# Expert tiles of 384 slots instead of 512, fifty of them instead of thirty-nine

## What is computed

```python
xn = layernorm(x)
# mixer: in-projection, causal convolution of 4 taps, silu, a linear recurrence along the sequence, out-projection
mixed = mixer(xn)
# experts: 8 of them, the best two for each token
logits = xt @ w_gate
top_logits, sel = top_k(logits, 2)
probs = softmax(top_logits)
h = silu(einsum('td,edh->eth', xt, w1)) * einsum('td,edh->eth', xt, w3)   # 128 -> 256
y = einsum('eth,ehd->etd', h, w2)                                         # 256 -> 128
out = einsum('ktd,tk->td', y[sel.T, t_idx], probs)
return x + mixed + out
```

## Time and profile before

| what | us |
|---|---|
| median of 3 runs | 543.55 (541.63 to 545.46) |
| the profiled execution, its own time | 539.55 |
| its span, first to last instruction | 537.7 |
| what lies around the span | 1.85 |

### The profile page before, as it was taken

How to read it: one execution, slowest core, us unless ns; L and a number is a source line. 1 busy time by engine, 2 the same in 40 slices (tenths; PEclk the granted TensorE clock), 3 DMA queues, 4 the chain that set the end, 5 groups by cost and what they waited for, 6 DMA issues and landing times.

```text
span 537.7 us, 8279 instructions
## 1 busy us (share of the span) xinstructions
PE 455.9 (85%) x2118; PEld 322.9 (60%) x2118; DVE 446.7 (83%) x947; ACT 313.6 (58%) x380; POOL 326.8 (61%) x317
## 2 busy tenths in 40 slices
PE   0668797778888889887999999999999998888863
PEld 0666663344434444444888888888888885444343
DVE  5898859899999999995977667667777765999996
ACT  1224236788888988886444444444444435888970
POOL 1047777788887868400477777777777777842210
PEclk9996668989999999998999999999999999899986
DMA  9501111951111111122466656666566640079995
GB/s 249 136 27 51 56 51 54 162 95 47 41 41 41 42 39 41 55 75 59 122 177 174 181 164 190 167 175 189 168 186 187 185 126 17 0 129 174 235 236 165
DMA packets 72599, 63.26 MB, mean 118 GB/s; under 512 B 9418, under 2 KB 64878, under 8 KB 72576
## 3 DMA queue, kind: packets, MB, share of 16 engines
q1 hardware_dynamic: 61184, 37.50, 27.1%
q0 software_dynamic: 11392, 25.53, 18.0%
HBM read 39.50 MB, written 25.31 MB: 121 GB/s over the span
## 4 chain that ended last, share of the span: by engine, by line
PE 45%; DVE 39%; issue 12%; ACT 3%; DMA 1%; DVEq 0%; SPq 0%; ACTq 0%
PE PD L593 13%; DVE acc L958 8%; PE PA L579 3%; DVE hbuf L917 3%; PE PA L583 3%; PE PA L580 3%; PE PB L579 3%; DVE ybuf L923 3%; PE PB L583 3%; PE PB L580 3%; DVE ybuf L929 3%; PE PD L566 3%; PE PC L452 3%; DVE gbuf L903 3%; DVE ebuf L945 3%
## 5 line engine op out<-in xcount | busy, mean ns | idle before, releaser
L397 POOL DMA_INDIRECT moe_out<-xnT,dst_u x156 | 162.4, 1041 | 85.9 <-DVE xnT L1131 43.8
L389 POOL DMA_INDIRECT moe_in<-xn,slot_u x128 | 148.1, 1157 | 71.5 <-issue 41.5
L1090 DVE TENSOR_TENSOR xn<-xn,PB 128x1024 f32<-128x1024 f32 x39 | 47.6, 1220 | 40.4 <-PE PB L583 40.4
L593 PE MATMUL PD<-xn 128*128 128x128 f32 x624 | 76.1, 275 | 0.9 <-DVE xnT L1131 0.9
L958 DVE SCALAR_TENSOR_TENSOR acc<-PA,cw,acc 128x510 f32<-128x510 f32 (+2 forms) x96 | 68.6, 734 | 7.7 <-ACT acc L694 7.5
L593 PEld LDWEIGHTS PD<-xn 128*128 128x128 f32 x624 | 72.8, 192 | 1.1 <-issue 1.0
L759 ACT ACTIVATE xn<-PA 128x1024 f32<-128x1024 f32 x39 | 40.1, 1028 | 38.6 <-PE PA L583 38.5
L512 PE MATMUL PA<-xnT,WinT 128*128 (+1 forms) x64 | 36.7, 702 | 28.1 <-DVE acc L958 27.1
L500 PE MATMUL PC<-xc,Wc 128*128 128x512 f32 x128 | 58.0, 596 | 2.6 <-ACT xc L735 2.6
L473 PE MATMUL PD<-xc,WgB 128*128 128x512 f32 x128 | 57.5, 592 | 0.0
L748 ACT ACTIVATE whi<-xn 128x512 fp32r<-128x512 f32 x39 | 24.6, 632 | 38.7 <-DMA xn<-in_L_ffn_w_dram 38.7
(11 more groups left out here) (149 smaller groups left out, 930.4 us busy)
## 6 DMA issues: line engine op xcount, KB each, us to landing
xn<-in_L_ffn_w_dram SPq DMA_DIRECT2D x117, 128.0 KB, 2.4
xn<-moe_in SPq DMA_DIRECT2D x39, 266.0 KB
xacc<-moe_out POOLq DMA_DIRECT2D x16, 512.0 KB, 7.6
out_dram<-xacc SPq DMA_DIRECT2D x7, 512.0 KB, 8.2
moe_out<-xnT,dst_u POOLq DMA_INDIRECT x156
moe_in<-zrow SPq DMA_DIRECT2D x8, 266.0 KB, 6.7
moe_in<-xn,slot_u POOLq DMA_INDIRECT x128, 2.4
xacc<-in_L_attn_x_dram SPq DMA_DIRECT2D x2, 512.0 KB, 4.6
```

Of the source, the lines that this page charges most:

```text
L389: gp.indirect_dma_start(xs_dram, bass.IndirectOffsetOnAxis(ap=slot_u[:, k, j:j + 1], axis=0), xn_row[:, j, :], None).then_inc(s_scat, 16)
L397: gp.indirect_dma_start(yt_dram, bass.IndirectOffsetOnAxis(ap=dst_u[:, t, j:j + 1], axis=0), yo[t % OUTS][:, j, :], None, bounds_check=PAI ...
L593: last = pe.matmul(PD[:, 512 + j * D:512 + (j + 1) * D], hid[b][:, k * SLOTS + j * P:k * SLOTS + (j + 1) * P], w2b[b][:, k * D:(k + 1) * D ...
L1090: ve.tensor_tensor(hid[b], sil, PB[:, :], ALU.mult).then_inc(s_hid, 1)
```

## The change

A tile has 384 slots, in 3 blocks of 128 rows (`TG`) instead of 4. The same formula for the number of tiles then gives (16384 + 8 * 383) // 384 = 50. The tables get longer (50 entries; 22 thresholds for each expert instead of 16), and a few scratch views move to other places. The halves of a tile's hidden values lie in one PSUM bank each, 384 columns of 512, and are read through a view with a gap. The number of tiles is even now, so the endings of the loops change. Core of the diff:

```diff
-SLOTS = 512
+SLOTS = 384
+TG = SLOTS // P
+MOST = -(-TOKENS // SLOTS)
 PAIRS = TOKENS * TOP_K
 MOE_TILES = (PAIRS + EXPERTS * (SLOTS - 1)) // SLOTS
...
+        def halved(t):
+            return t.rearrange("p (c s) -> p c s", c=HALVES)
+
+        def in_banks(ps):
+            return ps[:, :].rearrange("p (c s) -> p c s", c=HALVES)[:, :, 0:SLOTS]
...
-            with sp.Fori(0, (MOE_TILES - 5) // 2) as i:
+            with sp.Fori(0, (MOE_TILES - 4) // 2) as i:
                 load_down(i * 2 + 2, 0, False)
                 load_up(i * 2 + 4, 0, False)
                 load_down(i * 2 + 3, 1, False)
                 load_up(i * 2 + 5, 1, False)
-            t = MOE_TILES - 3
+            t = MOE_TILES - 2
             load_down(t, 0, False)
-            load_up(t + 2, 0, False)
             load_down(t + 1, 1, False)
-            load_down(t + 2, 0, False)
...
-                for j in range(GT):
+                for j in range(TG):
                     gp.indirect_dma_start(yt_dram, bass.IndirectOffsetOnAxis(ap=dst_u[:, t, j:j + 1], axis=0),
...
-                for j in range(GT):
+                for j in range(TG):
                     last = pe.transpose(PD[:, j * P:(j + 1) * P], xs[b][:, j, 0:D], ident[:, :])
...
-                    out_c = [ps[:, c_ * SLOTS:(c_ + 1) * SLOTS] for c_ in range(HALVES)]
+                    out_c = [ps[:, c_ * GROUP:c_ * GROUP + SLOTS] for c_ in range(HALVES)]
...
-                for j in range(GT):
+                for j in range(TG):
                     for k in range(HALVES):
                         last = pe.matmul(PD[:, 512 + j * D:512 + (j + 1) * D],
...
-            t = MOE_TILES - 1
+            t = MOE_TILES - 2
             up(t, 0, False)
-            down(t - 1, (t - 1) // 2, 1, False)
+            transp(t + 1, t // 2, 1, False)
+            down(t - 1, t // 2 - 1, 1, False)
+            up(t + 1, 1, False)
             down(t, t // 2, 0, False)
+            down(t + 1, t // 2, 1, False)
...
-                act.activation(xhi[:, b, :], PD[:, 0:512], ACT.Copy).then_inc(s_xhi, 1)
+                act.activation(xhi[:, b, :], PD[:, 0:SLOTS], ACT.Copy).then_inc(s_xhi, 1)
...
-                act.activation(sil, PA[:, :], ACT.Silu).then_inc(s_sil, 1)
+                act.activation(halved(sil), in_banks(PA), ACT.Silu).then_inc(s_sil, 1)
...
-                ve.tensor_tensor(xlo[:, b, :], PD[:, 0:512], xhi[:, b, :].bitcast(F32), ALU.subtract).then_inc(s_xlo, 1)
+                ve.tensor_tensor(xlo[:, b, :], PD[:, 0:SLOTS], xhi[:, b, :].bitcast(F32), ALU.subtract).then_inc(s_xlo, 1)
...
-                ve.tensor_tensor(hid[b], sil, PB[:, :], ALU.mult).then_inc(s_hid, 1)
+                ve.tensor_tensor(halved(hid[b]), halved(sil), in_banks(PB), ALU.mult).then_inc(s_hid, 1)
...
-                ve.tensor_tensor(yo[ring], PD[:, 512:1024].rearrange("p (j d) -> p j d", j=GT),
-                                 slot_p[:, b, :].unsqueeze(2).broadcast_to([P, GT, D]), ALU.mult).then_inc(s_yc, 1)
+                ve.tensor_tensor(yo[ring], PD[:, 512:512 + TG * D].rearrange("p (j d) -> p j d", j=TG),
+                                 slot_p[:, b, :].unsqueeze(2).broadcast_to([P, TG, D]), ALU.mult).then_inc(s_yc, 1)
```

More of the change, by code:

```diff
@@ L82, in block_kernel @@
         src_i = sb("src_i", [P, MOE_TILES], I32)
-        dst_u = sb("dst_u", [P, MOE_TILES, GT], U32)
+        dst_u = sb("dst_u", [P, MOE_TILES, TG], U32)
         pad_i = sb("pad_i", [P, EXPERTS], I32)
@@ L90, in block_kernel @@
         tile_r = sb("tile_r", [P, MOE_TILES])
-        mine = sb("mine", [P, GT, TOP_K])
-        part = sb("part", [P, GT, TOP_K])
-        slot_p = sb("slot_p", [P, 2, GT])
+        mine = sb("mine", [P, TG, TOP_K])
+        part = sb("part", [P, TG, TOP_K])
+        slot_p = sb("slot_p", [P, 2, TG])
         acc = sb("acc", [P, HALVES, GROUP])
@@ L118, in block_kernel @@
         w2b = [in_xn(1024 + 256 * b, 256) for b in range(2)]
[L119 to L122, removed]
+        xs = [in_xn(1536 + TG * ROW * b, TG * ROW).rearrange("p (j r) -> p j r", j=TG) for b in range(2)]
+        sil = in_xn(2600, HALVES * SLOTS)
+        hid = [in_xn(3624 + 1024 * b, HALVES * SLOTS) for b in range(2)]
+        yo = [xnT[:, GROUP * b:GROUP * b + SLOTS].rearrange("p (j d) -> p j d", j=TG) for b in range(OUTS)]
         def flat(t):
@@ L139, in block_kernel @@
         ones64 = flat(al[:, :, :])[:, 640:704]
-        thr = flat(al[:, :, :])[:, 704:832].rearrange("p (e m) -> p e m", e=EXPERTS)
+        thr = flat(ybuf[:, :, :])[:, 0:EXPERTS * MOST].rearrange("p (e m) -> p e m", e=EXPERTS)
         rev = flat(al[:, :, :])[:, 832:840]
@@ L146, in block_kernel @@
         eid_f = flat(al[:, :, :])[:, 920:920 + MOE_TILES]
-        row_f = flat(al[:, :, :])[:, 960:960 + MOE_TILES]
+        row_f = flat(al[:, :, :])[:, 704:704 + MOE_TILES]
         skip = flat(al[:, :, :])[:, 1000:1008]
@@ L170, in block_kernel @@
         den = gbuf[:, 1, 384:448]
[L171 to L174, removed]
+        cmp_m = flat(xc[:, 2, :, :])[:, 0:EXPERTS * MOST].rearrange("p (e m) -> p e m", e=EXPERTS)
+        cmp_t = flat(xc[:, 2, :, :])[:, 192:192 + MOE_TILES * EXPERTS].rearrange("p (t e) -> p t e", e=EXPERTS)
+        cmp_s = flat(xc[:, 2, :, :])[:, 600:600 + MOE_TILES * EXPERTS].rearrange("p (t e) -> p t e", e=EXPERTS)
+        tail = flat(ybuf[:, :, :])[:, 256:256 + MOE_TILES]
         PA, PB, PC, PD = pb("PA"), pb("PB"), pb("PC"), pb("PD")
@@ L330, in _ @@
                 sp.dma_start(xs_dram[bass.ds(row, SLOTS), :].rearrange("(j p) d -> p j d", p=P),
-                             zrow[:, :, :].broadcast_to([P, GT, ROW])).then_inc(s_fill, 16)
+                             zrow[:, :, :].broadcast_to([P, TG, ROW])).then_inc(s_fill, 16)
             sp.wait_ge(s_fill, 16 * EXPERTS)
@@ L400, in _ @@
             for b in range(OUTS):
-                gp.wait_ge(s_ys[b], 16 * GT * len(range(b, MOE_TILES, OUTS)))
+                gp.wait_ge(s_ys[b], 16 * TG * len(range(b, MOE_TILES, OUTS)))
             for pair in range(0, BLOCKS, 2):
@@ L608, in _ @@
             down(0, 0, 0, True)
-            with pe.Fori(0, (MOE_TILES - 3) // 2) as i:
+            with pe.Fori(0, (MOE_TILES - 4) // 2) as i:
                 up(i * 2 + 2, 0, False)
@@ L779, in _ @@
             round_x(3, 1)
-            with act.Fori(0, (MOE_TILES - 5) // 2) as i:
+            with act.Fori(0, (MOE_TILES - 4) // 2) as i:
                 tile_step(i * 2 + 3, i + 1, 1, True)
                 tile_step(i * 2 + 4, i + 2, 0, True)
-            t = MOE_TILES - 2
-            tile_step(t, t // 2, 1, True)
-            tile_step(t + 1, (t + 1) // 2, 0, False)
+            t = MOE_TILES - 1
+            tile_step(t, t // 2, 1, False)
             mixer(act, mix, STEPS_A, GROUPS + 2)
@@ L1015, in _ @@
             ve.wait_ge(s_cst, 13)
-            ve.tensor_copy(thr, iot[:, 0:128].rearrange("p (e m) -> p e m", e=EXPERTS))
-            ve.tensor_copy(rev, iot[:, 128:128 + EXPERTS])
+            ve.tensor_copy(thr, iot[:, 0:EXPERTS * MOST].rearrange("p (e m) -> p e m", e=EXPERTS))
+            ve.tensor_copy(rev, iot[:, 176:176 + EXPERTS])
             ve.tensor_copy(tix, iot[:, 256:256 + MOE_TILES])
             ve.tensor_copy(reg0, iot[:, 320:320 + EXPERTS])
-            ve.tensor_copy(xn_row[:, :, HOME], iot[:, 136:136 + TILES])
+            ve.tensor_copy(xn_row[:, :, HOME], iot[:, 184:184 + TILES])
             link(ve.memset(zrow[:, :, :], 0.0))
-            ve.tensor_copy(zrow[:, 0, HOME:HOME + 1], iot[:, 200:201]).then_inc(s_zrow, 1)
+            ve.tensor_copy(zrow[:, 0, HOME:HOME + 1], iot[:, 248:249]).then_inc(s_zrow, 1)
             ve.wait_ge(s_zrow, 1)
@@ L1044, in _ @@
             cnt = inc[:, TILES - 1, :]
-            link(ve.tensor_tensor(cmp_m, thr, cnt.unsqueeze(2).broadcast_to([P, EXPERTS, 16]), ALU.is_lt))
+            link(ve.tensor_tensor(cmp_m, thr, cnt.unsqueeze(2).broadcast_to([P, EXPERTS, MOST]), ALU.is_lt))
             link(ve.reduce_sum(nte, cmp_m, AX_X))
@@ L1129, in scale_y @@
                 if used is not None:
-                    ve.wait_ge(s_ys[ring], used * (16 * GT))
-                ve.tensor_tensor(yo[ring], PD[:, 512:1024].rearrange("p (j d) -> p j d", j=GT),
-                                 slot_p[:, b, :].unsqueeze(2).broadcast_to([P, GT, D]), ALU.mult).then_inc(s_yc, 1)
+                    ve.wait_ge(s_ys[ring], used * (16 * TG))
+                ve.tensor_tensor(yo[ring], PD[:, 512:512 + TG * D].rearrange("p (j d) -> p j d", j=TG),
+                                 slot_p[:, b, :].unsqueeze(2).broadcast_to([P, TG, D]), ALU.mult).then_inc(s_yc, 1)
             def tile_step_v(t, n, b, ring, used, early=False, last=False):
```

10 lines of the change are left out of this document (5 added, 5 removed).

## The result

| | median us | runs |
|---|---|---|
| before | 543.68 | 541.63 to 545.46, 4 runs |
| changed kernel | 568.21 | 566.20 to 570.47, 4 runs |
| ratio | 1.0459 | 95% interval 1.0425 to 1.0493 |

The change makes the kernel 24.5 us slower (23.1 to 26.8 by the interval); 564 was predicted, with 553 to 573 as range. The chip has a second, slower state that some executions fall into: ratios and intervals here are of the fast executions alone, medians of all, so a ratio need not be the quotient of the medians beside it. The profiled execution of the changed kernel took 570.47 us (span 568.6), the slowest of its four, while that of the kernel before was faster than the three runs it stands beside, so the two traces lie 30.9 us apart.

A forecast was written before the change was run, and what follows sets the result against it. SP's issuing, 4.43 us a tile for 50 tiles, was taken to bound the expert stage: 539.55 + 21.9 + 0.6 (tables) = 562 us for the profiled execution, put at 564 between that and 566 from the median; range 553 to 573.

The forecast's parts named there:

- SP binds: Expert stage: SP's unchanged program takes 4.43 us a tile, over PE's 3.80, so SP ends last; chance 0.73.
- PE's step: Expert stage, PE's transposes, down and up matmuls for one tile: from 5.00 to 3.80 us (3.75 to 4.46).
- matmuls don't get shorter: Rival: up matmuls of 384 columns still take 0.238 us, PE's step 4.46 us, tying with SP; 564 to 566 us, chance 0.10.
- Start of SP's loop: Opening of the expert stage: shorter PE work starts SP's loop 2.1 us earlier, at 257.3 instead of 259.35 us.
- Tail: End of the expert stage: last weights issued at 459.2 us, up(49) starts at 463.1, mixer at 469.8.
- The ring: Expert stage, not forecast: rows, transposes, down matmuls, SP's wait and next loads close a loop, 8.45 us for two tiles.
- Tables: Small tables on DVE ahead of the mixer: 540 more elements at 1.04 ns, 0.6 us more (0 to 1).
- Behind the experts: Mixer after the expert stage: nothing changes, cost 0 us (bounds -1 and +1).
- The sum: Whole kernel: 539.55 + 21.9 (expert stage) + 0.6 (tables) = 562 us for the profiled execution; 564 predicted.
- SP keeps up: Rival: SP's loop steps can go at 3.92 us, so PE bounds; 539 us, near 536 below 3.93; chance 0.10.
- POOL binds: Rival, shared with transfers: scatters crowded to 1.55 us, three take 4.65 a tile; 10 us more, 572; joint chance 0.07.
- transfers bind: Rival, shared with POOL: eleven more sets of weights crowd the scatters; 10 us more, 572 us; joint chance 0.07.

The follow-up runs named there:

- A: The changed kernel, 50 tiles of 384 slots, without further edits: 568.21 us.
- the first remedy: One table entry fewer per tile against the changed kernel, load_down taking the expert from a register load_up left: 557.52 us.
- the four experiments on the undisturbed chip: Changed kernel with one table entry more 600.92 us, one fewer 557.52, no range checks 544.55; kernel before with one entry more 550.18.
- B: The kernel before the change, 39 tiles of 512 slots: median 543.68 us beside the changed kernel, 542.92 beside the first four experiments.

## Why the prediction was right, point by point

- *SP binds.* Right, and shown: its wait vanished, an entry more costs its full price in A, three checks fewer give 23.7 us back. SP's step was predicted as 4.43 us by one subtraction, 5.00 - 16.5 / 29, and is 4.46 over 45 steps. The Trainium skill, "DMA: Bandwidth & Descriptors", Latency and other measured facts, gives about 600 ns as the floor of a tensor_load. Here the instruction itself takes 0.27 us; with index and check a read added to the loop costs 0.75 us and one taken out gives back 0.53 to 0.56. The estimate of 3.3 us a tile from that figure was too low by a quarter.
- *PE's step.* Predicted 3.80, measured 3.84 where PE binds again. Twelve up matmuls with the bubbles at their edges were put at 12 x 0.183 us; in the tail above they take 474.25 - 472.08 = 2.17 us, 0.181 each (0.174 from start to start inside a half). The rival "matmuls don't get shorter" is out.
- *Start of SP's loop.* Predicted 2.1 us less of opening work. From the first transposes to the first L331 of the loop it was 259.35 - 246.2 = 13.2 us and is 263.37 - 252.1 = 11.3, 1.9 less.
- *Tail.* Too short. From L331 of tile 47 to the mixer the sum gave 13.1 us, it took 478.89 - 464.13 = 14.8. The step followed the weights' path only, L319 and 2.4 us of landing. The rows come later: issued at 467.11, waited for until 470.44. The transposes wait for them and down(47) stands between them and up(49), which starts at 472.08 instead of about 470.4. This is the same wait for rows that the stage shows throughout, and it is a part of the ring found later.
- *The ring.* Not in the prediction. It said that the two buffers of each kind only let engines run ahead. True while SP's own step is the longest, but the ring of rows, transposes, down, `load_down` and `load_up` has only two tiles in it, 8.45 us. In A's steady part it cost nothing (SP waits 0.3 us in 150), but it took more than half of the gain of the first remedy: 10.7 us for 26.
- *Tables.* From the first of their operations to the mixer, DVE needs 97.97 - 91.78 = 6.2 us instead of 95.37 - 89.75 = 5.6: 0.6, as predicted.
- *Behind the experts.* 568.6 - 478.89 = 89.7 us, 537.7 - 447.93 = 89.8 before. Nothing, as predicted.
- *The sum.* From the first transposes to the mixer the stage takes 478.89 - 252.1 = 226.8 us, 447.93 - 246.2 = 201.7 before: 25.1 more, where the prediction had 21.9. The 3.2 us it missed are 1.4 of step (45 x 0.03), 1.7 of tail and 0.2 of start, all to the same side. The predicted 22.5 us on the median of before give 566, 2 under the measured 568.21. The point, 564, lay 2 lower still, because the prediction split the 4 us by which the profiled execution lay under the median. Those 4 us lie ahead of the stage: of the 5.9 us by which A's first transposes come later only 0.6 are the tables, and in the four experiments on the undisturbed chip they begin at 249.8 to 251.1 us, at 250.9 in B with one more entry, whose tables are the old ones. So the profiled execution of B, at 246.2, was an early one, and the rest is most likely not the change's; one trace with the old tables is all that speaks for it.
- *SP keeps up, POOL binds, transfers bind.* None of them. POOL waits for DVE 18.5 us from 282 to 432 us, and DVE for POOL not at all. The transfers move 171 GB/s in A, and 199 where the checks are left out, so they weren't what held A.

## What to carry to other kernels

An engine that only issues transfers shows no busy time, so its slack has to be read from its waits: step less wait is its own work for a tile, and that doesn't shrink when the tile does. Making tiles smaller divides the arithmetic and multiplies what is fixed for a tile, here three table reads at 0.5 to 0.75 us and four issues at 0.4 to 0.6. Before counting on a fixed cost that is taken out again, look for the ring just under it, and ask of each edit whether it stands inside that ring or beside it.

## What was not expected of the hardware

- A value read from a table into a register costs SP far more than the 0.27 us that the read itself shows: 0.75 us of step when one was added to A's loop, 0.53 to 0.56 when one was taken out. Leaving out the three range checks alone brought a step of 4.42 down to 3.86, of which 0.2 is wait, so some 0.25 us a check.
- The rows of a tile (199.5 KB in pieces of 532 bytes) land 3.1 us after their issue by the page of the changed kernel, and in the trace with one entry fewer PE starts on them 3.3 us after it; the loads of 128 KB land after 2.1.
- Up matmuls follow each other at 0.174 us with 384 columns, 0.232 to 0.238 with 512: between these two lengths the cost goes by the columns.
- Where PE is busy 90% of the time with gaps of 0.3 to 1.6 us in each step, the granted clock stays at 1.00.
